# Attention and expert layers in one pipelined kernel: scores in three units of 512 columns, value products in two fills, Exps and Gelus of a batch kept apart

## What is computed

```python
# block 1: a plain attention over 128 features, reduced to its row sums
att = softmax(q @ k.T * 128**-0.5); y = einsum('bqk,bvd->bqd', att, v)    # sum of att times sum of v
out1 = layernorm(xn + y @ w_fc.T + b_fc) * gamma + beta
# block 2: 16 heads of 8 features, causal
h = rms(xn, n1_w)
q, k, v = heads(h @ wq.T), heads(h @ wk.T), heads(h @ wv.T)
q, k = rms(q, qn_w), rms(k, kn_w)
ao = softmax(causal(q @ k.T * 8**-0.5)) @ v
x1 = xn + mask(ao @ wo.T)
xf = rms(x1, n2_w)
wts = top 2 of softmax(xf @ gate_w.T) over 4 experts, normalised
moe = wts[0]*o0 + wts[1]*o1 + wts[2]*o2 + wts[3]*o3      # o0: gelu(xf@e0_up)@e0_down
                                                         # o1: (silu(xf@w1)*(xf@w2))@down
                                                         # o2: three gelu layers and a last one
                                                         # o3: two gelu layers and a last one
out2 = x1 + mask(moe)                                    # mask: the first 32 features are set to 0
```

## Time and profile before

| | |
|---|---|
| three runs | 232.12, 230.88, 232.77 us (median 232.12) |
| profiled execution, first to last instruction | 231.3 us |
| busy | PE 202.3, PE weight loads 145.6, DVE 160.1, ACT 160.1, POOL 112.9 us |
| mean granted clock of PE | 0.991 |

### The profile page before, as it was taken

How to read it: one execution, slowest core, us unless ns; L and a number is a source line. 1 busy time by engine, 2 the same in 40 slices (tenths; PEclk the granted TensorE clock), 3 DMA queues, 4 the chain that set the end, 5 groups by cost and what they waited for, 6 DMA issues and landing times.

```text
span 231.3 us, 6236 instructions
## 1 busy us (share of the span) xinstructions
PE 202.3 (87%) x2132; PEld 145.6 (63%) x2132; DVE 160.1 (69%) x608; ACT 160.1 (69%) x310; POOL 112.9 (49%) x227
## 2 busy tenths in 40 slices
PE   0542898859999999999999999999999999997883
PEld 0311455436867787678767776867686777766563
DVE  2245059795858897789868995899489667847704
ACT  2123447745989698978898789878987998732730
POOL 3834225872572747282837282737375437506000
PEclk9999999997999999999999999999999999999999
DMA  4900100000000020002000200020000000100000
GB/s 124 389 16 11 37 3 1 4 0 0 4 0 3 3 68 6 0 3 68 0 3 6 68 4 0 3 68 4 0 3 27 23 4 0 48 0 3 23 0 27
DMA packets 7570, 6.09 MB, mean 26 GB/s; under 512 B 624, under 2 KB 7024, under 8 KB 7536
## 3 DMA queue, kind: packets, MB, share of 16 engines
q1 hardware_dynamic: 7248, 5.44, 7.5%
q10 hardware_dynamic: 288, 0.21, 0.3%
HBM read 4.60 MB, written 1.05 MB: 24 GB/s over the span
## 4 chain that ended last, share of the span: by engine, by line
PE 73%; DVE 11%; issue 5%; ACT 4%; POOL 3%; DMA 2%; SPq 0%; POOLq 0%; ACTq 0%; DVEq 0%
PE even_ps L1357 12%; PE scores_ps L1242 10%; PE pv_ps L1271 7%; PE odd_ps L1343 7%; PE a_ps L1212 6%; PE even_ps L1343 5%; PE even_ps L1387 4%; PE odd_ps L1387 3%; PE odd_ps L1369 3%; PE a_ps L1184 3%; PE pv_ps L1275 3%; PE a_ps L1286 3%; DMA first<-in_first 2%; DVE acc L1054 2%; PE a_ps L1202 2%
## 5 line engine op out<-in xcount | busy, mean ns | idle before, releaser
L325 POOL TENSOR_SCALAR_AFFINE_SELECT probs<-probs 128x512 f32<-128x512 f32 x64 | 40.3, 635 | 47.4 <-ACT probs L507 46.7
L507 ACT ACTIVATE probs<-scores_ps 128x768 f32<-128x768 f32 x64 | 49.9, 809 | 5.1 <-PE scores_ps L1242 4.9
L1242 PE MATMUL scores_ps<-qT,kT 32*128 32x128 f32 (+1 forms) x512 | 31.4, 361 | 0.3 <-ACT probs L507 0.2
L1357 PE MATMUL even_ps<-l_h,mid 128*128 128x256 f32 x128 | 30.7, 383 | 1.0 <-ACT l_h L569 1.0
L1242 PEld LDWEIGHTS scores_ps<-qT,kT 32*128 32x128 f32 x512 | 24.2, 192 | 10.4 <-issue 9.1
L1357 PEld LDWEIGHTS even_ps<-l_h,mid 128*128 128x128 f32 x128 | 23.4, 190 | 6.2 <-ACT l_h L569 2.1
L1343 PE MATMUL odd_ps<-xfT,up 128*128 128x256 f32 x80 | 22.1, 391 | 0.4 <-DVE acc L1054 0.4
L1271 PE MATMUL pv_ps<-probs,v_aug 128*32 128x256 f32 x256 | 21.3, 406 | 0.9 <-DVE pv_rows L834 0.4
L569 ACT ACTIVATE l_h<-even_ps 128x512 f32<-128x512 f32 x24 | 14.5, 606 | 8.1 <-PE even_ps L1357 7.1
L1212 PE MATMUL a_ps<-qkvT,xnT 128*128 128x384 f32 x32 | 17.5, 635 | 2.1 <-ACT qkv L543 1.5
L1343 PE MATMUL even_ps<-xfT,up 128*128 128x256 f32 x64 | 18.8, 418 | 0.0
(11 more groups left out here) (150 smaller groups left out, 451.4 us busy)
## 6 DMA issues: line engine op xcount, KB each, us to landing
x_sb<-in_x SPq DMA_DIRECT2D x8, 128.0 KB, 2.5
acc<-in_x SPq DMA_DIRECT2D x8, 128.0 KB, 2.1
out<-acc SPq DMA_DIRECT2D x8, 128.0 KB, 1.9
mid<-in_mid SPq DMA_DIRECT2D x1, 640.0 KB, 7.5
up<-in_up SPq DMA_DIRECT2D x1, 578.0 KB, 6.4
downs<-in_down SPq DMA_DIRECT2D x1, 512.0 KB, 8.3
first<-in_first SPq DMA_DIRECT2D x1, 320.0 KB, 5.5
row<-in_rows ACTq DMA_DIRECT2D x1, 200.0 KB, 5.2
```

Source lines behind the costliest of these rows:

```text
L325: nc.gpsimd.affine_select(out=own, in_=own, compare_op=ALU.is_ge, fill=0.0, base=0, pattern=[[0, 2 * TILES], [1, P]], channel_multiplier=- ...
L507: nc.scalar.activation(probs[g % 2][:, 2 * half:2 * half + 2, 0:SEQ + P], scores_ps[:, 2 * half:2 * half + 2, 0:SEQ + P], ACT.Exp).then_in ...
L1242: ins = T.matmul(ps, kT[p][rows, g, kt * P:(kt + 1) * P], qT[p][rows, kt * P:SEQ], start=kt == 0, stop=kt == 1 and not searching, tile_pos ...
L1357: ins = T.matmul(ps_of(fill)[:, m * SEQ:(m + 1) * SEQ], wT[:, at_col:at_col + P], src[:, ci, :], start=(ci == 0), stop=(ci == HC - 1))
```

## The change

- q and k change parts. `kT` now holds k once, `qT` holds four copies of q, each masked to one head of a lane (`q_copy`, `q_rows`). One stationary k serves all groups.
- Scores come in three units of 512 columns for each lane: unit 0 is the first 128 keys with groups 0 and 1 (2x256 columns), unit 1 the last 128 keys with all four groups (4x128), unit 2 the first 128 keys with groups 2 and 3. Each is one matmul for a lane. `exp_unit` takes two lanes of a unit, 1024 elements; `probs` has three buffers instead of two.
- Value products come in two fills, PV0 and PV1, of two groups each; `pv_turn` transposes 512 columns. PV0 needs units 0 and 1, PV1 unit 2.
- All scores of a batch, with their Exps and masks, are in slot n+2. Before, group 0 and parts of group 1 were worked on in slot n+1. In ACT's slot the Exps, the tanh and the gate's Exp stand together, then the Gelus.
- The queues of all engines are reordered: on PE, DVE, ACT and POOL as the diff shows, on SP the store comes after `load_x` and before `load_acc`. The pv bank has the fills XFT, PV0, GATE, PV1, WO.
- On DVE `qk_square` to the Newton steps are called with t-1 at the head of the slot, before with t near its end; the steps of `down` with t-4 instead of t-3.

```diff
 BANK_FILLS = {
-    "pv": (("PV0", 2), ("XFT", 3), ("GATE", 3), ("PV1", 2), ("PV2", 2), ("PV3", 2), ("WO", 2)),
+    "pv": (("XFT", 3), ("PV0", 2), ("GATE", 3), ("PV1", 2), ("WO", 2)),
...
-    UNITS = HALVES * GROUPS
+    PAIRS = GROUPS // 2
+
+    SCORE_UNITS = [(0, range(0, 2)), (1, range(GROUPS)), (0, range(2, 4))]
+    UNITS = len(SCORE_UNITS)
+    EXPS = HALVES * UNITS
...
-        qT = [sb(f"qT{p}", [P, SEQ]) for p in range(2)]
-        kT = [sb(f"kT{p}", [P, GROUPS, SEQ]) for p in range(2)]
+        qT = [sb(f"qT{p}", [P, GROUPS, SEQ]) for p in range(2)]
+        kT = [sb(f"kT{p}", [P, SEQ]) for p in range(2)]
...
-        probs = [sb(f"probs{g}", [P, LANES, TILES * SEQ]) for g in range(2)]
+        probs = [sb(f"probs{u}", [P, LANES, TILES * SEQ]) for u in range(UNITS)]
...
-            for t in range(BATCHES + 3):
+            for t in range(SLOTS):
                 load_x(t)
+                store(t - 4)
                 load_acc(t - 2)
-                store(t - 3)
...
             def slot(t):
+                mask(t - 2, 0)
                 h0_gamma(t - 3)
-                mask(t - 2, 3)
+                mask(t - 2, 1)
                 v_copy(t - 1)
                 h0_beta(t - 3)
+                mask(t - 2, 2)
+                mask(t - 2, 3)
                 h0_add(t - 3)
+                ln_variance(t)
+                ln_pow(t)
                 mask(t - 2, 4)
                 mask(t - 2, 5)
-                mask(t - 2, 6)
-                mask(t - 2, 7)
-                ln_variance(t)
-                ln_pow(t)
                 h_square(t)
                 h_mean(t)
-                x1_add(t - 3)
                 h_eps(t)
                 h_pow(t)
+                x1_add(t - 3)
+                x1_start(t - 2)
+                h0_variance(t - 2)
+                h0_scale(t - 2)
                 biased(t - 1)
-                h0_variance(t - 2)
-                x1_start(t - 2)
-                h0_scale(t - 2)
-                mask(t - 1, 0)
-                mask(t - 1, 1)
                 x1_variance(t - 2)
                 x1_pow(t - 2)
-                mask(t - 1, 2)
...
             def exp_unit(n, u):
                 if not live(n):
                     return
-                g, half = divmod(u, HALVES)
-                wait(act, "scores_full", GROUPS * n + g + 1)
-                fill_ready(act, f"PV{(g - 2) % GROUPS}", n if g >= 2 else n - 1)
-                nc.scalar.activation(probs[g % 2][:, 2 * half:2 * half + 2, 0:SEQ + P],
-                                     scores_ps[:, 2 * half:2 * half + 2, 0:SEQ + P], ACT.Exp).then_inc(s["exp_done"], 1)
+                unit, half = divmod(u, HALVES)
+                wait(act, "scores_full", UNITS * n + unit + 1)
+                fill_ready(act, "PV0" if unit == 0 else "PV1", n - 1)
+                nc.scalar.activation(probs[unit][:, 2 * half:2 * half + 2, :], scores_ps[:, 2 * half:2 * half + 2, :], ACT.Exp
+                                     ).then_inc(s["exp_done"], 1)
...
             def slot(t):
+                exp_unit(t - 2, 0)
+                qkv_copy(t - 1, 1)
+                exp_unit(t - 2, 1)
+                q0_copy(t - 1)
+                exp_unit(t - 2, 2)
+                exp_unit(t - 2, 3)
+                a0_softmax(t - 2, 0)
+                xf_copy(t - 3)
                 exp_unit(t - 2, 4)
                 exp_unit(t - 2, 5)
                 e1_tanh(t - 3)
                 a0_softmax(t - 2, 1)
                 gate_exp(t - 3)
-                exp_unit(t - 2, 6)
-                exp_unit(t - 2, 7)
                 gelu(t - 3, "L1", l1_h, ("L2",))
                 gelu(t - 3, "E0", e0_h, ("DN0", "DN1"))
-                q_copy(t - 1)
-                k_copy(t - 1, 0)
-                k_copy(t - 1, 1)
-                k_copy(t - 1, 2)
-                k_copy(t - 1, 3)
+                k_copy(t - 1)
+                q_copy(t - 1, 0)
+                q_copy(t - 1, 1)
+                q_copy(t - 1, 2)
+                q_copy(t - 1, 3)
                 gelu(t - 3, "L2", l2_h, ("L3",))
                 gelu(t - 3, "D3", d3_h, ("U3",))
                 x_copy(t)
-                exp_unit(t - 1, 0)
-                qkv_copy(t, 0)
-                exp_unit(t - 1, 1)
-                gelu(t - 3, "L3", l3_h, ("DN0", "DN1"))
-                qkv_copy(t, 1)
-                gelu(t - 3, "U3", u3_h, ("DN0", "DN1"))
                 x1_square(t - 2, 0)
                 x1_square(t - 2, 1)
-                exp_unit(t - 1, 2)
-                q0_copy(t)
-                exp_unit(t - 1, 3)
-                xf_copy(t - 2)
-                a0_softmax(t - 1, 0)
+                gelu(t - 3, "L3", l3_h, ("DN0", "DN1"))
+                qkv_copy(t, 0)
+                gelu(t - 3, "U3", u3_h, ("DN0", "DN1"))
...
             def slot(t):
+                find_maxima(t - 2)
+                residual_scale(t - 3)
+                qk_square(t - 1)
+                qk_mean(t - 1)
+                rsqrt_input(t - 1)
+                rsqrt_halve(t - 1)
+                rsqrt_guess(t - 1)
+                down(t - 4, 0, 0)
+                newton_square(t - 1, 0)
+                down(t - 4, 0, 1)
+                newton_error(t - 1, 0)
+                down(t - 4, 0, 2)
+                newton_correct(t - 1, 0)
+                down(t - 4, 0, 3)
+                newton_square(t - 1, 1)
+                newton_error(t - 1, 1)
+                newton_correct(t - 1, 1)
+                newton_square(t - 1, 2)
+                newton_error(t - 1, 2)
+                down(t - 4, 1, 0)
+                newton_correct(t - 1, 2)
+                down(t - 4, 1, 1)
+                qk_norm(t - 1)
+                down(t - 4, 1, 2)
+                ln_statistics(t)
+                down(t - 4, 1, 3)
+                ln_moments(t)
+                a0_max(t - 2, 0)
+                pv_turn(t - 2, 0)
+                ln_normalise(t)
+                logits_copy(t - 3)
+                gate_finite(t - 3)
+                e1_gate(t - 3)
+                gate_number(t - 3)
+                a0_max(t - 2, 1)
...
                 e1_product(t - 3)
-                qk_norm(t - 1)
                 h0_sum(t - 2)
...
-            def scores(n, g):
+            def scores(n, u):
...
-                for kt in range(TILES):
-                    for lane in range(LANES):
-                        rows = slice(32 * lane, 32 * lane + 32)
-                        ps = scores_ps[:, lane, 0:SEQ] if kt == 0 else scores_ps[:, lane, SEQ:SEQ + P]
-                        ins = T.matmul(ps, kT[p][rows, g, kt * P:(kt + 1) * P], qT[p][rows, kt * P:SEQ],
-                                       start=kt == 0, stop=kt == 1 and not searching, tile_position=(32 * lane, 0))
+                for lane in range(LANES):
+                    rows = slice(32 * lane, 32 * lane + 32)
+                    out_ps = scores_ps[:, lane, :].rearrange("p (g q) -> p g q", q=width)
+                    ins = T.matmul(out_ps, kT[p][rows, kt * P:(kt + 1) * P], qT[p][rows, groups.start:groups.stop, queries],
+                                   start=True, stop=not searching, tile_position=(32 * lane, 0))
...
             def slot(t):
+                find_maxima(t - 2)
+                scores(t - 2, 0)
                 qkv_project(t - 1, 1)
+                down(t - 4, 0)
+                q0_project(t - 1)
                 scores(t - 2, 1)
-                weigh_v(t - 2, 0)
-                q0_project(t - 1)
-                down(t - 4, 0)
                 down(t - 4, 1)
                 a0_scores(t - 2, 0)
                 xf_turn(t - 3)
                 scores(t - 2, 2)
+                weigh_v(t - 2, 0)
+                up_layer(t - 3, "E1A", e1T[:, 0:HID])
                 gate(t - 3)
-                up_layer(t - 3, "E1A", e1T[:, 0:HID])
                 a0_scores(t - 2, 1)
-                weigh_v(t - 2, 1)
-                scores(t - 2, 3)
                 up_layer(t - 3, "E1B", e1T[:, HID:])
                 fc_row(t - 2)
-                weigh_v(t - 2, 2)
+                weigh_v(t - 2, 1)
                 up_layer(t - 3, "L1", l1T)
                 up_layer(t - 3, "E0", e0uT)
                 qk_turn(t - 1)
                 square_layer(t - 3, "L2", l2T, l1_h, "L1")
                 up_layer(t - 3, "D3", e3dT)
-                weigh_v(t - 2, 3)
                 x_turn(t)
-                find_maxima(t - 1)
-                scores(t - 1, 0)
+                wo_project(t - 2)
+                square_layer(t - 3, "L3", l3T, l2_h, "L2")
                 qkv_project(t, 0)
-                square_layer(t - 3, "L3", l3T, l2_h, "L2")
                 e3_up_layer(t - 3)
-                wo_project(t - 2)
```

More of the change, by code:

```diff
@@ L575, in q_copy @@
                 fill_ready(act, "QKT", n)
-                wait(act, "scores_full", GROUPS * (n - 1))
-                nc.scalar.copy(qT[n % 2][:], ps_of("QKT")[:, 0:SEQ])
-            def k_copy(n, g):
+                wait(act, "scores_full", UNITS * (n - 1))
```

(26 more changed lines are left out.)

128 lines of the change are left out of this document (52 added, 76 removed).

## The result

| | before | after |
|---|---|---|
| median (lowest to highest) | 231.50 (230.54 to 232.77) us | 288.24 (286.95 to 289.53) us |
| ratio, 95% interval | | 1.250 (1.242 to 1.257) |
| profiled span | 231.3 us | 287.8 us |
| mean granted clock of PE | 0.991 | 0.917 |

The change makes the kernel 25% slower. I had forecast slower, by the mechanism that the profile shows, but 266 us with a range that ended at 275: 22 us too little.

The account below looks back on a forecast made before the run. PE was taken to bound the kernel before. Span 231.3 + 28.6 (first slots 2.3, slots 4 to 8 24.0, slot 9 3.6, end -1.3) + 6 for the clock = 265.9; with 0.8 to the median, 266 us said, range 250 to 275.

Parts of the forecast that it names:

- What bounds the kernel: PE bounds the old slot (busy 23.70 of 23.8 us); in the new slot it idles 4.2 us.
- PE's own work: Per slot, three larger score units save 0.24 us and two pair fills 0.30, together 0.5 less on PE.
- Step 1: Slot start: ACT's Gelu of U3, table load, one Exp and qkv_copy(t-1,1) done 3.5 us after U3's end.
- Step 2: DVE, after qkv_copy: a0_max(t-2,0) queues behind square, Newton steps, layer norm and eight downs, a chain of 8.4 us.
- Step 3: ACT's softmax, xf_copy and hand-overs take 1.2 us; PE's first value fill starts 13.1 after U3's end.
- W: Start of weigh_v(B,0), PE's first value fill, B being batch t-2, counted from the end of U3: 13.1 us.
- Step 4: PE from the first value fill to U3's end: 15.5 us, 0.8 of it waiting at FC; slot 28.6 against 23.8.
- The clock: PE's clock falling behind the gaps in slots 3 to 9: 1.7 us each, between 0 and 12, 6 taken.
- rival (273): Clock lost in every slot: the full 12 us for PE's gaps, 273 us in all; chance 0.25.
- The first slots: qkv_project(2,0) in slot 2 some 1.5 us later than before; slot 3 ends at about 71.7, +2.3.
- Slot 9 and the end: Slot 9, without Newton chain: 23.6 against 20.0, +3.6 us; end, with wo_project before L3 and U3: -1.3.
- Faster: Rival: PE stays the bound, if a0_max(t-2,0) is done 4.2 us after qkv_copy; 227 us, chance 0.05.

Follow-up runs that it names:

- runs 1 to 3: Against the changed kernel: a0_max(t-2,0) earlier on DVE, 265.6 us; a0_softmax(t-2,0) later on ACT, 266.8. Against the kernel before: both a0_max behind the last Newton step, 259.7.
- run 7: Changed kernel with its units, fills and table loads kept, but DVE, ACT, PE and POOL queues reordered: 240.1 us, ratio 1.030.
- run 5: Changed kernel with v_copy, h0_gamma, h0_beta and h0_add moved behind ln_pow on POOL: 280.0 us, ratio 1.209.
- run 4: Changed kernel with the score matmuls of unit 2 written five times in batches 1 to 6: 277.4 us, ratio 1.193.
- runs 7 and 8: The changed kernel with reordered queues, 240.1 us; the same with a second round of moves, 240.5 us, ratio 1.038.

## Why the prediction was wrong in size, point by point

The mechanism came as forecast; two terms of the sum were too small. A slot at full clock takes 30.6 us and not 28.6, 1.2 of it since DVE's chain takes 9.7 and not 8.4, the rest behind the first value fill. And the fallen clock costs 11.5 us in slots 3 to 8, not the 6 that I had allowed, with some more in slot 2.

- **What bounds the kernel; that PE would idle behind `a0_max`.** Right, and runs 1 to 3 show it: the wait is PE's longest, in front of the first value fill, and put down to ACT's `xfT`; two different single moves each remove it; the same move makes a like one, in front of S01, in the kernel before.
- **PE's own work, -0.5 a slot.** The pieces were right: 1.08 for a unit (145.41 to 146.49), 1.44 for a pair fill at full clock. Over a slot PE's busy time falls by 0.2 only (run 7), and in the kernel after none of it lies on the path.
- **Step 1, `qkv_copy` done at 3.5.** 3.51.
- **Step 2, the chain of 8.4.** It took 9.68. Mis-sized: the 1.1 for POOL was an average over the Newton steps of the kernel before; in the new place gamma, beta, `v_copy`, `h0_add` and two masks of 1024 stand beside them, and the chain's instructions are together 2.6 us longer than quiet ones (0.95, 0.89 and 0.55 in three Newton steps of 0.22, 0.47, 0.31 and 0.67 in three others of 0.20). Run 5 shows 1.0 of it for the first four of POOL's calls. What I should have asked is which of POOL's instructions the new place meets, one by one, and not what the old place met on average.
- **Step 3, W = 13.1.** 14.3 (159.73 less 145.41), all of it from step 2, the hand-overs being 0.2 shorter. The idle time is 5.2, not 4.2.
- **Step 4, 15.5 behind W.** 17.3 in a shorter slot, of which 1.0 is the clock, and 19.1 in a longer, of which 2.8. Run 4, with the clock at 1.00, has 16.2: PE reaches FC at 5.7 behind W instead of 5.0, since `gate_number`, which I had left out, stands between `e1_gate` and `a0_max(B,1)` on DVE and takes 0.68 in that run (157.69 to 158.37). The slot without loss of clock is 30.56 against my 28.6.
- **The clock, 6 between 0 and 12.** It was 11.5 in slots 3 to 8 alone (run 4). With one gap in the trace before, I took half; but the gap forecast was twice as long as the one that had shown the loss, in every slot, and nothing in the trace spoke for a slot that would escape. The upper bound was the likely value, and that rival (273) would have been the better forecast; but it too is 15 short. Run 4, at full clock in slots 4 to 8, takes 277.4 us, above my whole range: the gap without any loss of clock was priced too low as well, by 8 us in these slots. The Trainium skill, "TensorE: Matmul & The Clock Gate", section "HAM oscillation", describes a loop with an idle stretch in each turn as one that falls back to the low clock in each turn. Here the trace agrees for slots 3 to 8: right behind the gap of each the granted clock is 0.50, as in the row of 160.00:162.00. Slot 9, with 0.9 us of idle time before its value fill, has 1.00 there.
- **The first slots.** `qkv_project(2,0)` ended 3.8 later than walked, and slot 3 took 31.4 against 26.5. Of slot 3's 4.9, run 4 gives 2.2 back as clock; the other 2.7 are not. For slot 2 I had no term for the clock, but it had fallen there as well. Windows of the kernel after (before, the first of them had 1.00):

```profile
24.00:50.00 26.00, 20.12 (x120) 8.37 (x124) 13.16 (x41) 12.06 (x25) 10.35 (x19) 0.88 0.02 6
50.00:80.00 30.00, 22.33 (x161) 13.87 (x154) 19.03 (x67) 15.69 (x33) 13.13 (x23) 0.88 0.01 2
```

  By an estimate from the first row, at most 26.0x0.12 = 3.1 of the 3.8 is clock. Two pieces of PE's work show 2.0 of it: the first value fill takes 2.72 (36.88 to 39.60) instead of 1.44, `qkv_project(2,0)` 1.55 (47.46 to 49.01) instead of 0.84. No run repeats matmuls in slot 2, so this part is not shown by an experiment. The column of the clock does not show all either: in both kernels matmuls run at half speed up to about 33 where it says 1.00 (before, a `qkv_project` takes 1.58 from 27.13).
- **Slot 9 and the end.** 24.0 against 23.6; 23.1 from U3's end on against 22.5.

The sum, on spans: slot 2 +3.8, slot 3 +4.9, slots 4 to 8 +17.2 (5x2.0 less a slot 8 that is 1.9 quicker, 7.9, and clock, 9.3), slot 9 +0.4, the end +0.6, less the 6 that I had allowed for the clock: +20.9 of the 21.9 between 265.9 and 287.8. The last 1.0 is slot 8 of the kernel before, which was shorter by that than a full one (187.5 less 69.4 is 118.1, not 5x23.8): the forecast had kept that, and 28.6 for each slot here does not.

**The rivals.** Clock lost in every slot came true, with a longer chain on top of it: the two errors were taken as alternatives, and the range as wide as one of them, where both have the same cause (the chain makes the gap, POOL makes the chain longer, the longer gap lets the clock fall) and add. "Faster" was rightly small: its condition, `a0_max` done 4.2 after `qkv_copy`, was missed by 5.6 us.

What stays open: of the 1.0 a slot that runs 7 and 8 keep over the kernel before, the waits are seen, but their common cause isn't shown. All Exps of a batch now lie in the first half of a slot, where the kernel before had begun four of eight in the slot before; that this is the reason is argued, not shown. Units, fills and the exchange of q and k were not run one by one.

## What to carry to other kernels

Before a call is moved in an in-order queue, ask what stands behind its *waiting* instruction on the other engine: here one reduction of 0.4 us, put behind a chain of 9 us, held a copy that had nothing to do with it, and cost 22 us of 288, the clock lost behind the gap included. Price the gap that comes of it with the clock in full once a shorter gap in the same trace has already lost it, and add the errors that make each other larger instead of choosing between them. A change of sizes that comes with a new order is best run in the old order, or the best one, too: here the kernel with the new sizes was 3% slower in the best order found, and 25% in its own.

## What the runs showed of the hardware

- **Useless work made the kernel faster.** Run 4's extra matmuls fill 3.4 of the 5.2 us of the gap, and take 11 us off the whole.
- **After the same gap the clock stays low for two different times, in turns.** In the slot of 31.6 us 3.8x0.43/0.5 = 3.3 us behind the gap are at half clock, by the third row; in the slot of 33.4 it stays low from 126.36 to about 135.7, 9.3 us, by the first and second. Windows of the kernel after:

```profile
126.50:134.50 8.00, 8.00 (x51) 5.24 (x49) 3.22 (x13) 3.38 (x7) 3.44 (x8) 0.50 0.13 35
135.50:144.00 8.50, 8.50 (x73) 6.71 (x66) 5.75 (x29) 4.86 (x15) 2.01 (x5) 0.99 0.00 0
159.80:163.60 3.80, 3.80 (x36) 2.21 (x36) 1.02 (x3) 1.70 (x2) 2.42 (x6) 0.57 0.26 72
```

- **A small operation of DVE can last as long as the POOL instruction beside it, and some do not.** In the kernel after, two masks of 1024 fill POOL from 152.28 to 154.42, 1.07 each. The Newton step that starts at 152.50 ends at 153.45, the next (153.59) at 154.48: each about 0.1 after a mask's end. In run 5 the same two ends are 147.60 and 148.67, and the steps end at 147.70 and 148.75. The `down` step between them, which reads PSUM, takes its usual 0.30. The Trainium skill, "SBUF — State Buffer", section "SBUF: two separate sides", says that an operation of DVE with two inputs in SBUF and one of GpSimd that reads SBUF exclude each other for the length of the instruction; the trace agrees. A step with one input can be drawn out as well (L872, 151.32 to 151.99 instead of 0.20, beside POOL's `h0_beta`, which ends at 151.93). The section could have told me that the chain's price beside POOL goes by the length of POOL's instructions.
- **A table load costs its 1.28 us and no more.** The Exp behind it starts 0.02 later (146.13, 147.43). "ScalarE: Activation LUTs" of the Trainium skill, section "What ACT_TABLE_LOAD costs", counts about 2.7 us for a switch; the trace has half of that, and the measurement decides.
